# A convolution stack with an FFT-domain layer: the last sums of an image pair, moved from VectorE alone to ScalarE, VectorE and GpSimd

## The chip, the cores and the metric

One core of a Trainium2 chip runs the whole kernel. The metric is the device time of one execution in microseconds (us). The kernel before was timed in three runs: median 3791.02 us, from 3787.89 to 3796.55. A further execution was profiled; it took 3767.42 us.

## The reference

The input is a batch of 32 samples, each with 16 channels of 256 x 256 fp32 values. Two layers follow each other, both of the form x + conv(group_norm(x)):

```python
x = x + _L0_conv_ref(_gn(x), L0_conv_weight_int8, L0_conv_scale_weight, L0_conv_bias)
x = x + _L1_conv_ref(_gn(x), L1_conv_w_real, L1_conv_w_imag, L1_conv_b_real, L1_conv_b_imag)
```

Layer 0 quantises the normalised input with one scale for the whole batch (the maximum over all samples) and convolves it 3 x 3. Layer 1 goes to the frequency domain, convolves there and comes back:

```python
X = jnp.fft.rfftn(x, axes=(-2, -1), norm='backward')
Xr, Xi = (jnp.real(X), jnp.imag(X))
Yr = _rconv(Xr, wr) - _rconv(Xi, wi) + b_real[:, None, None]
Yi = _rconv(Xr, wi) + _rconv(Xi, wr) + b_imag[:, None, None]
return jnp.fft.irfftn(lax.complex(Yr, Yi), axes=(-2, -1), norm='backward')
```

## The kernel before, in words

**Layout.** The 128 partitions hold 16 channels x 8 rows. A sample is 32 blocks of 8 rows, `img[u]` (two samples in SBUF, u = 0 or 1). Two blocks make a pair, so a sample has 16 pairs (`PAIRS`).

**Setup** (about the first 680 us). Sums, squares, maxima and minima of all samples give the batch scale; GpSimd builds the weights meanwhile.

**Main stage.** `periods` runs one period per sample s, and a period has 16 slots, t = 0 to 15. In slot t each engine does its part for pairs that are at different stages:

- TensorE (PE), in this order: `turn_pair(t+4)` transposes a folded pair (L963); `dft_pair(t+3)` transforms it along the row (L972); for the next sample `row_means` (L1030) and `conv_pair` of layer 0 (L1017, L1019), of which `CONV_OF` gives slots 0 to 3 one pair, slots 4 to 9 two, and slots 10 to 15 none; `mix_pair(t+1)` applies the frequency-domain weights (L985) from `stack`; `finish_pair(t)` brings the pair back to pixels in `fin_ps` (L999, L1004), with the part that is even about the row's middle (the cosine part) in `fin_ps[:, :, 0, :]` and the odd one (the sine part) in `fin_ps[:, :, 1, :]`. In slots 4 to 9 `row_means` and `conv_pair` stand once before `mix_pair` and once behind it.
- ScalarE (ACT): `turn_out(t+4)` evicts the transposes (L540), `x_high(t+3)` the high half of the spectrum into `xn` (L547), `scale_pair` (L533), `y_high(t+1)` (L554), and `store(t-2)`, two DMAs to `out` from ACT's own queue (L562).
- VectorE (DVE): `y_low(t)` (L827), `x_low(t+3)` (L821), `layer0_pair` (L834, then statistics L836), `round_pair` (L813, L815), `finish_pair(t)` (L844 to L849).
- GpSimd (POOL): `fold(t+4)` (L729 to L732), which may run two turns ahead of PE.
- The SyncE queue (SP): `load_pair(t-3)` of the sample after next into the rows that `store` has emptied (it waits for the store's landing, L461), `restack(t+3)` (four DMAs xn to stack, L454), and `halo_rows` in slots 2, 6, 10 and 14 (L443).

**The end of a pair.** `near` are the columns 0 to 127 of the pair's rows, `far` the columns 255 down to 128. near gets even + odd, far gets even - odd. VectorE does it with four operations of 128 x 256 each, all on PSUM and `img`. The last raises `done_s`, for which PE's next `finish_pair` waits (there is one `fin_ps`), and `store` on ScalarE.

**Once per sample.** The statistics of the next sample pass through slots 10 and 11: DVE L855 and L857, PE `group_stat` (L1046) twice, DVE L870, POOL L741, DVE L877 (`zb_s`), for which `fold(16)` waits. In slots 12 to 15 the edge rows are transformed: ACT L582, L583, PE `dft_rows` (L1054, behind `finish_pair(13)`), ACT L586, DVE `row_low` (L883), PE `mix_rows` (L1065, slot 14), ACT L571, DVE L889, PE `finish_rows` (L1075), ACT L590, L591.

Each engine runs its own list in the order in which it is written; between engines there are only semaphores.

## Time and profile before

| what | before |
|---|---|
| three timed runs, median (lowest to highest) | 3791.02 us (3787.89 to 3796.55) |
| the profiled execution | 3767.42 us, span 3765.6 us |
| PE busy, instructions | 2979.5 us (79%), 45732 |
| DVE busy | 3117.7 us (83%), 5880 |
| ACT busy | 1893.1 us (50%), 2799 |
| POOL busy | 1490.4 us (40%), 1984 |
| 16 DMA engines, mean rate | 194 GB/s, 730.98 MB |
| granted TensorE clock | 0.99 of full speed |

Busy shares are means over the setup, in which PE has nothing to do, and the main stage. A busy PE is counted while a matmul is in its pipeline. The clock is full in the whole main stage.

### The profile page before, as it was taken

What the parts mean: (1) busy time and instruction counts of PE and PEld (TensorE: products, weight loads), DVE (VectorE), ACT (ScalarE), POOL (GpSimd) and SP (SyncE); (2) the same over time, 40 slices, a digit from 0 to 9 for tenths busy, and PEclk for the clock granted to TensorE, in tenths of its full rate; (3) what the DMA queues carried; (4) which work ended last, traced back from release to release, by engine and by line L of the source; (5) the groups of instructions that cost most, each with busy time, mean ns of one, the idle gap of its engine ahead of it and who ended that gap; (6) DMA issues with size and microseconds to landing.
All of it is one profiled execution on the core that took longest, in us unless ns stands there. A gap on an engine that the chain in (4) does not pass through costs nothing.

```text
span 3765.6 us, 126495 instructions
## 1 busy us (share of the span) xinstructions
PE 2979.5 (79%) x45732; PEld 2646.9 (70%) x45732; DVE 3117.7 (83%) x5880; ACT 1893.1 (50%) x2799; POOL 1490.4 (40%) x1984
## 2 busy tenths in 40 slices
PE   0000004899999999999999989999999999999998
PEld 0000002788888888888888878888888888888888
DVE  8999994688878888888888878888888888888876
ACT  8999981344444444444444434444444444444443
POOL 4777000344334344343343334333433433333444
PEclk9999999999999999999999999999999999999999
DMA  8767650366666666666666656666666666666655
GB/s 309 241 236 242 236 188 16 118 196 198 198 188 196 197 195 197 194 192 195 199 194 191 195 178 194 194 192 195 192 194 191 196 192 194 193 199 191 198 179 179
DMA packets 630696, 730.98 MB, mean 194 GB/s; under 512 B 76752, under 2 KB 602160, under 8 KB 614736
## 3 DMA queue, kind: packets, MB, share of 16 engines
q1 hardware_dynamic: 482640, 588.71, 48.6%
q10 hardware_dynamic: 147456, 134.28, 12.7%
q8 instruction: 374, 6.13, 0.7%
q14 instruction: 226, 1.85, 0.2%
HBM read 262.58 MB, written 134.22 MB: 105 GB/s over the span
## 4 chain that ended last, share of the span: by engine, by line
PE 50%; SPq 16%; issue 11%; DMA 11%; DVE 9%; ACT 1%; POOL 1%; ACTq 1%; DVEq 0%; POOLq 0%
PE y_ps L985 12%; PE mean_b L1030 10%; SPq L454 9%; PE conv_ps L1017 7%; PE x_ps L972 6%; DMA stack<-xn 5%; PE fin_ps L1004 5%; SPq L376 4%; PE t_ps L963 3%; DMA out<-img 3%; PE conv_ps L1019 3%; DVE scaled L758 2%; DMA img<-in_x 2%; PE fin_ps L999 2%; DVE scaled L759 1%
## 5 line engine op out<-in xcount | busy, mean ns | idle before, releaser
L729 POOL TENSOR_SCALAR eo<-img,norm 128x256 f32<-128x256 f32 x512 | 481.5, 940 | 1502.1 <-PE t_ps L963 1274.2
L985 PEld LDWEIGHTS y_ps<-mix_w,stack 128*128 128x128 f16 x24576 | 787.5, 99 | 158.1 <-DMA stack<-xn 84.6
L985 PE MATMUL y_ps<-mix_w,stack 128*128 128x64 f16 x24576 | 810.4, 194 | 62.4 <-DMA stack<-xn 62.0
L540 ACT ACTIVATE xt<-t_ps 128x512 f32<-128x512 f32 x512 | 305.8, 597 | 910.8 <-PE t_ps L963 802.9
L554 ACT ACTIVATE y_hi<-y_ps 128x512 f16<-128x512 f32 x512 | 305.8, 597 | 535.4 <-PE y_ps L985 534.4
L834 DVE SCALAR_TENSOR_TENSOR img<-conv_ps,cst,img 128x512 f32<-128x512 f32 x512 | 382.3, 747 | 226.9 <-PE conv_ps L1019 226.4
L821 DVE SCALAR_TENSOR_TENSOR xn<-x_ps,norm,xn 128x512 f16<-128x512 f32 x512 | 383.1, 748 | 220.7 <-ACT xn L547 215.6
L1030 PE MATMUL mean_b<-row_mean,img 128*128 128x48 f32 x4096 | 538.2, 275 | 16.6 <-DVE img L834 16.2
L972 PE MATMUL x_ps<-dft,xt 128*128 128x128 f32 x4096 | 543.0, 276 | 0.0
L1030 PEld LDWEIGHTS mean_b<-row_mean,img 128*128 128x128 f32 x4096 | 511.3, 196 | 31.7 <-DVE img L834 31.5
L972 PEld LDWEIGHTS x_ps<-dft,xt 128*128 128x128 f32 x4096 | 499.7, 192 | 0.1
L547 ACT ACTIVATE xn<-x_ps,norm 128x512 f16<-128x512 f32 x512 | 352.4, 688 | 231.0 <-DMA stack<-xn 145.3
L533 ACT ACTIVATE scaled<-img,b,a 128x512 f32<-128x512 f32 x512 | 412.0, 805 | 106.1 <-DVE quant L813 71.1
L1004 PE MATMUL fin_ps<-inv,y_hi 128*128 128x128 f16 x4096 | 459.1, 221 | 0.0
L951 PE MATMUL misc_ps<-im_f,group 128*128 128x32 f32 x2 | 0.6, 396 | 575.5 <-DVE im_f L779 575.5
L1017 PE MATMUL conv_ps<-quant,conv_w 128*128 128x512 bf16 x1536 | 427.2, 388 | 25.6 <-DMA halo<-quant 25.5
L951 PEld LDWEIGHTS misc_ps<-im_f,group 128*128 128x128 f32 x2 | 0.5, 310 | 575.5 <-issue 575.5
L1004 PE MATMUL fin_ps<-inv,y_lo 128*128 128x128 f16 x2048 | 400.6, 221 | 0.0
L1004 PEld LDWEIGHTS fin_ps<-inv,y_hi 128*128 128x128 f16 x4096 | 358.8, 99 | 39.6 <-issue 0.2
L730 POOL TENSOR_TENSOR eo<-img 128x256 f32<-128x256 f32 x512 | 381.1, 744 | 0.0
L732 POOL TENSOR_TENSOR eo<-eo,img 128x256 f32<-128x256 f32 x512 | 376.2, 735 | 0.0
L836 DVE BATCH_NORM_STATS2 bn<-img 128x6 f32<-128x512 f32 x512 | 355.6, 694 | 17.6
(134 smaller groups left out, 5138.9 us busy)
## 6 DMA issues: line engine op xcount, KB each, us to landing
stack<-xn SPq DMA_DIRECT2D x2048, 132.0 KB, 2.6
img<-in_x SPq DMA_DIRECT2D x1024, 128.0 KB, 2.8
out<-img ACTq DMA_DIRECT2D x1024, 128.0 KB, 3.0
img<-in_x SPq DMA_DIRECT2D x120, 1024.0 KB, 4.9
halo<-quant SPq DMA_DIRECT2D x192, 193.3 KB, 3.3
halo<-quant SPq DMA_DIRECT2D x64, 169.1 KB, 3.0
row_mean<-table_row_mean SPq DMA_DIRECT2D x1, 768.0 KB, 15.4
spread<-table_spread SPq DMA_DIRECT2D x1, 512.0 KB, 14.4
```

What stands on the lines that cost most here:

```text
L533: nc.scalar.activation(scaled[:], img[u][:, 2 * j:2 * j + 2, :], ACT.Identity, bias=b0[:, bass.ds(k, 1)], scale=a0[:, bass.ds(k, 1)]).then ...
L729: nc.gpsimd.tensor_scalar(even, rows[:, :, 0:F], norm[v][:, 2:3], None, ALU.add).then_inc(shift_s, 1)
L730: nc.gpsimd.tensor_tensor(odd, rows[:, :, 0:F], rows[:, :, N - 1:F - 1:-1], ALU.subtract)
L732: nc.gpsimd.tensor_tensor(even, even, rows[:, :, N - 1:F - 1:-1], ALU.add).then_inc(fold_s, 1)
L821: nc.vector.scalar_tensor_tensor(natural(t, 1), x_ps[:].rearrange("p q b k -> p (q b) k"), norm[v][:, 4:5], natural(t, 0), ALU.mult, ALU.s ...
L834: nc.vector.scalar_tensor_tensor(rows, conv_ps[:], out_scale, rows, ALU.mult, ALU.add).then_inc(x1_s, 1)
L836: nc.vector.bn_stats(bn[:, c, :], rows).then_inc(bn_s, 1)
L972: last = nc.tensor.matmul(x_ps[:, q, b, :], xt[:, t % 2, b, q, :], dft[:, q, :], start=True, stop=True)
L985: last = nc.tensor.matmul(y_ps[t % 2][:, g, b, :], stack[:, t % 2, g, first:first + F], mix_w[:, 2 * at + b, g, f, part, :], start=i == 0, ...
L1004: last = nc.tensor.matmul(fin_ps[:, b, q, :], y[:, t % 2, 2 * b + q].rearrange("p x g -> p (x g)"), inv[:, q, part, :], start=False, stop= ...
L1017: nc.tensor.matmul(conv_ps[:], conv0_w[:, dw, :], quant[:, 2 * c:2 * c + 2, dw:dw + N], start=dw == 0, stop=False)
L1030: nc.tensor.matmul(mean_ps[half], img[u][:, hb, F * half:F * half + F], row_mean[:, hb, :], start=False, stop=False)
```

## The change

ScalarE gets a new operation behind `y_high`, in front of `store`: `odd_out(t)` waits for `finish_pair(t)` of PE and copies the odd part, scaled, from `fin_ps` to SBUF (`odd_part`, four buffers). VectorE adds the even part to near and far (two operations) and now waits for that copy. GpSimd does near + odd and far - odd of pair t-2 behind `fold(t+4)`, and raises `done_s`. PE's next `finish_pair` waits for the copy (`odd_s`) and for VectorE (`even_s`), no longer for `done_s`.

```diff
+        odd_part = sb("odd_part", [P, 4, 2, F])
...
+            def odd_out(s, t):
+
+                act.wait_ge(fin_s, done(s, t))
+                act.wait_ge(done_s, done(s, t - 4))
+                nc.scalar.activation(odd_part[:, t % 4], fin_ps[:, :, 1, :], ACT.Copy, scale=1.0 / FIN).then_inc(odd_s, 1)
...
+                    if mix:
+                        odd_out(s, t)
                     if mix and t >= 2:
                         store(s, u, t - 2)
...
+            def unfold(s, u, t):
+
+                rows, odd = img[u][:, 2 * t:2 * t + 2, :], odd_part[:, t % 4]
+                near, far = rows[:, :, 0:F], rows[:, :, N - 1:F - 1:-1]
+                pool.wait_ge(even_s, done(s, t))
+                pool.sem_inc(tick_s, 1)
+                pool.wait_ge(odd_s, done(s, t))
+                pool.sem_inc(tick_s, 1)
+                nc.gpsimd.tensor_tensor(near, near, odd, ALU.add)
+                nc.gpsimd.tensor_tensor(far, far, odd, ALU.subtract).then_inc(done_s, 1)
...
                     if runs(mix, conv, t + 4):
                         fold(s, u, t + 4)
+                    if mix and t >= 2:
+                        unfold(s, u, t - 2)
+                    if later(s, mix) and t < 2:
+                        unfold(s - 1, 1 - u, t + PAIRS - 2)
...
+            for t in (PAIRS - 2, PAIRS - 1):
+                unfold(samples - 1, 1, t)
...
-                even, odd = fin_ps[:, :, 0, :], fin_ps[:, :, 1, :]
-                dve.wait_ge(fin_s, done(s, t))
-                nc.vector.scalar_tensor_tensor(near, even, 1.0 / FIN, near, ALU.mult, ALU.add).then_inc(even_s, 1)
+                even = fin_ps[:, :, 0, :]
+                dve.wait_ge(odd_s, done(s, t))
+                nc.vector.scalar_tensor_tensor(near, even, 1.0 / FIN, near, ALU.mult, ALU.add)
                 nc.vector.scalar_tensor_tensor(far, even, 1.0 / FIN, far, ALU.mult, ALU.add).then_inc(even_s, 1)
-                dve.wait_ge(even_s, 2 * (PAIRS * s + t) + 1)
-                nc.vector.scalar_tensor_tensor(near, odd, 1.0 / FIN, near, ALU.mult, ALU.add)
-                dve.wait_ge(even_s, 2 * (PAIRS * s + t) + 2)
-                nc.vector.scalar_tensor_tensor(far, odd, -1.0 / FIN, far, ALU.mult, ALU.add).then_inc(done_s, 1)
...
                 pe.wait_ge(ylo_s, done(s, t))
-                pe.wait_ge(done_s, done(s, t - 1))
+                pe.wait_ge(even_s, done(s, t - 1))
+                pe.wait_ge(odd_s, done(s, t - 1))
```

What stands on ScalarE in a row where slots 4 to 9 follow each other, before (`scaled` is the pair for the quantisation, `xt` the transposes, `y_hi` the mixed spectrum's high half):

```order
L533 ACTIVATE scaled<-img,b,a 128x512 [waits rounded_s]
L554 ACTIVATE y_hi<-y_ps 128x512 [waits fin_s,mix_s]
L562 ISA [waits done_s]
L562 DMA out<-img 16x8x256
L562 ISA
L562 DMA out<-img 16x8x256
L538 REGISTER_ALU
L540 ACTIVATE xt<-t_ps 128x512 [waits dft_s,t1_s]
```

and now:

```order
L534 ACTIVATE scaled<-img,b,a 128x512 [waits rounded_s]
L555 ACTIVATE y_hi<-y_ps 128x512 [waits fin_s,mix_s]
L561 ACTIVATE odd_part<-fin_ps 128x256 [waits done_s,fin_s]
L569 ISA [waits done_s]
L569 DMA out<-img 16x8x256
L569 ISA
L569 DMA out<-img 16x8x256
L539 REGISTER_ALU
L541 ACTIVATE xt<-t_ps 128x512 [waits dft_s,t1_s]
```

The two DMAs of the store stood behind the wait for `mix_s` alone; now they stand behind a wait for `fin_s` too, which is the end of PE's slot.

The same engine in slot 13, now, where the edge rows of the next sample pass (`row_n` waits for `dft_rows`, which PE does behind `finish_pair(13)`):

```order
L555 ACTIVATE y_hi<-y_ps 128x512 [waits fin_s,mix_s]
L593 ACTIVATE row_n<-misc_ps,norm 48x2x128 [waits rowx_s]
L561 ACTIVATE odd_part<-fin_ps 128x256 [waits done_s,fin_s]
L569 ISA [waits done_s]
L569 DMA out<-img 16x8x256
```

`odd_part` is new there, behind `row_n`; the store already stood behind `row_n` before.

VectorE in slots 13 and 14, now (the odd copy gives `odd_s`):

```order
L871 SCALAR_TENSOR_TENSOR img<-fin_ps,img 128x2x128 [waits odd_s]
L872 SCALAR_TENSOR_TENSOR img<-fin_ps,img 128x2x128
L854 TENSOR_TENSOR y_lo<-y_ps,y_hi 128x512 [waits yhi_s]
L906 SCALAR_TENSOR_TENSOR row_n<-misc_ps,norm,row_n 48x2x128 [waits rowxh_s]
L848 SCALAR_TENSOR_TENSOR xn<-x_ps,norm,xn 128x4x128 [waits xhi_s]
```

Four additions on `fin_ps` have become two, and the first of them waits for ScalarE instead of PE.

## Rows read from the trace of the kernel before

**Rows 1.** Busy time by window: slot 5 of a sample; slots 10 to 15
```profile
1600.47:1607.57 7.10, 7.10 (x102) 6.12 (x100) 6.01 (x13) 2.58 (x4) 2.30 (x3) 1.00 0.50 154
1630.94:1662.74 31.80, 27.38 (x501) 25.58 (x500) 23.83 (x64) 15.69 (x30) 16.29 (x21) 1.00 0.62 188
```
(The columns are: us; then busy us of PE, PEld, DVE, ACT, POOL; clock; DMA share; GB/s.)

**Rows 2.** Who waited for whom, 768 to 3700 us: total, times, longest
```profile
PE y_ps L985 <- DMA stack<-xn: 57.9, 61, 2.4
PE t_ps L963 <- POOL eo L732: 47.6, 31, 1.7
PE misc_ps L1046 <- DVE small L857: 33.7, 30, 1.1
```

**Rows 3.** The SyncE queue's own waits, whole span
```profile
SPq L462 <- DMA out<-img: 166.9, 161, 2.9
```

**Rows 4.** Timeline of slot 5 (slots 6 to 9 alike): start, us, what
```profile
1600.47 0.22 PE L1004 MATMUL fin_ps<-inv,y_lo 128*128 128x128 f16 x1
1601.17 0.60 ACT L540 ACTIVATE xt<-t_ps 128x512 f32<-128x512 f32 x1 [2.51 <-PE t_ps L963]
1601.23 0.41 DVE L844 SCALAR_TENSOR_TENSOR img<-fin_ps,img 128x256 f32<-128x256 f32 x1
1602.06 0.69 ACT L547 ACTIVATE xn<-x_ps,norm 128x512 f16<-128x512 f32 x1 [0.30 <-PE x_ps L972]
1602.55 0.68 DVE L827 TENSOR_TENSOR y_lo<-y_ps,y_hi 128x512 f16<-128x512 f32 x1
1603.14 0.75 DVE L821 SCALAR_TENSOR_TENSOR xn<-x_ps,norm,xn 128x512 f16<-128x512 f32 x1
1603.80 0.75 DVE L834 SCALAR_TENSOR_TENSOR img<-conv_ps,cst,img 128x512 f32<-128x512 f32 x1
1604.93 0.64 PEld L1030 LDWEIGHTS mean_b<-row_mean,img 128*128 128x128 f32 x5
1605.16 0.60 ACT L554 ACTIVATE y_hi<-y_ps 128x512 f16<-128x512 f32 x1 [1.71 <-PE y_ps L985]
1605.36 1.27 ACTq L562 DMA_DIRECT2D out<-img  x2
```

**Rows 5.** Timeline of a slot in which DVE was late
```profile
1589.94 0.74 DVE L834 SCALAR_TENSOR_TENSOR img<-conv_ps,cst,img 128x512 f32<-128x512 f32 x1
1590.74 0.41 PEld L1030 LDWEIGHTS mean_b<-row_mean,img 128*128 128x128 f32 x3 [0.77 <-DVE img L834]
```

**Rows 6.** Timeline, PE in slots 10 and 12: the statistics
```profile
1632.36 0.61 PE L1046 MATMUL misc_ps<-small,group 128*128 128x1 f32 x4 [1.12 <-DVE small L857]
...
1640.90 0.55 PE L963 MATMUL t_ps<-ident,eo 128*128 128x128 f32 x3 [1.56 <-POOL eo L732]
```

**Rows 7.** Timeline of slots 13 and 14: the edge rows
```profile
1650.35 0.42 DVE L844 SCALAR_TENSOR_TENSOR img<-fin_ps,img 128x256 f32<-128x256 f32 x1 [0.24 <-PE fin_ps L1004]
1651.36 0.47 ACT L586 ACTIVATE row_n<-misc_ps,norm 48x256 f16<-48x256 f32 x1 [1.30 <-PE misc_ps L1055]
1652.28 0.47 DVE L883 SCALAR_TENSOR_TENSOR row_n<-misc_ps,norm,row_n 48x256 f16<-48x256 f32 x1
1652.81 1.19 PE L1065 MATMUL misc_ps<-image_w,row_n 48*128 48x96 f16 x24
1653.00 0.60 ACT L540 ACTIVATE xt<-t_ps 128x512 f32<-128x512 f32 x1 [1.17 <-PE x_ps L972]
1653.49 0.68 ACT L547 ACTIVATE xn<-x_ps,norm 128x512 f16<-128x512 f32 x1
1654.21 0.75 DVE L821 SCALAR_TENSOR_TENSOR xn<-x_ps,norm,xn 128x512 f16<-128x512 f32 x1 [1.46 <-ACT xn L547]
```

**Rows 8.** Groups by line: shape, count, busy, mean ns of one, idle before
```profile
L732 POOL TENSOR_TENSOR eo<-eo,img 128x256 f32<-128x256 f32 x512 | 376.2, 735 | 0.0
L591 ACT ACTIVATE im_f<-misc_ps 128x128 f32<-128x128 f32 x32 | 8.6, 269 | 0.0
```

**Rows 9.** Timeline, DVE beside a busy POOL
```profile
1644.38 0.70 DVE L815 TENSOR_SCALAR quant<-quant 128x512 bf16<-128x512 bf16 x1
```

More of the change, by code:

```diff
@@ L295, in build @@
             "images_s"))
-        fold_s, t1_s, t1e_s, dft_s, xhi_s, xlo_s, mix_s, yhi_s, ylo_s, fin_s, even_s, done_s = (sem(n) for n in (
-            "fold_s", "t1_s", "t1e_s", "dft_s", "xhi_s", "xlo_s", "mix_s", "yhi_s", "ylo_s", "fin_s", "even_s", "done_s"))
+        fold_s, t1_s, t1e_s, dft_s, xhi_s, xlo_s, mix_s, yhi_s, ylo_s, fin_s, even_s, odd_s, done_s = (sem(n) for n in (
+            "fold_s", "t1_s", "t1e_s", "dft_s", "xhi_s", "xlo_s", "mix_s", "yhi_s", "ylo_s", "fin_s", "even_s", "odd_s", "done_s"))
         shift_s = sem("shift_s")
@@ L495, in _ @@
             act.sem_inc(p1_act, 8)
-            for q in (t1e_s, xhi_s, yhi_s):
+            for q in (t1e_s, xhi_s, yhi_s, odd_s):
                 act.sem_inc(q, LEAD)
@@ L607, in _ @@
             pool.sem_inc(fold_s, LEAD)
+            pool.sem_inc(done_s, LEAD)
             setup = Tally(pool, setup_p)
@@ L744, in _ @@
             periods(pool, period)
+            for t in (PAIRS - 2, PAIRS - 1):
+                unfold(samples - 1, 1, t)
         @block.vector
         def _(dve):
-            for q in (xlo_s, ylo_s, done_s, x1_s):
+            for q in (xlo_s, ylo_s, even_s, x1_s):
                 dve.sem_inc(q, LEAD)
```

## The prediction

> **What bounds the kernel now.** I read the page first: PE and DVE are both near 80% busy, with no work for PE in the setup. So shares do not decide, and I went to windows, waits and timelines of one sample (some 97 us, 16 slots).
>
> In a slot with two conv pairs PE is busy for all of its 7.10 us and DVE for 6.01 [rows 1]: PE is the bound there, six slots in sixteen, and a faster DVE buys nothing. In slots 10 to 15 PE is busy for 27.38 of 31.80 us: the idle time that can be won lies there and in the slots just behind. Its largest parts are waits for the restacked spectrum, 57.9 us in total, for the first fold of the next sample, 47.6, and for the first statistic, 33.7 [rows 2]. Only the last two hang on DVE. The first hangs on SP, which itself stood 166.9 us waiting for stores to land before it could load [rows 3]. So the whole idle time of PE that any change could win is about 140 us, and what DVE can give is a part of 81.
>
> Call F the moment at which PE's `finish_pair` is done. In rows 4 it is 1600.47 + 0.22 plus 0.04 = 1600.73.
>
> **The change part by part.**
>
> *VectorE* loses two of four additions. Four take 1602.55 - 1601.23 = 1.32 us from start to start, so two free 0.66 us a slot [rows 4]. But the first now waits for ScalarE's copy. No row shows a copy of 256 PSUM columns; 128 take 269 ns [rows 8] and 512 take 0.60 us [rows 4], and between these I take 0.38. Copy from F to F + 0.38, VectorE at F + 0.42: before, it began at F + 0.50, held by other work. So in long slots the wait costs nothing and `y_low` starts at F + 1.1 instead of F + 1.82.
>
> *ScalarE's queue.* This is where I expect the cost. `store` was issued behind `y_high`: in rows 4 at 1605.36, while ScalarE had nothing to do until the next slot's transposes. Now it is issued behind the copy, so at F + 0.2, and `turn_out` stands behind it. The store's two DMA issues take 1.27 us [rows 4]; from the operation ahead of a store to the `turn_out` behind it pass 1653.00 - 1651.36 = 1.64 us [rows 7]. So `turn_out` starts at F + 1.65, where it started at F + 0.44 [rows 4].
> What is queued behind it: `x_high` 0.49 later [rows 7], at F + 2.14; `x_low` on VectorE 0.72 behind that [rows 7], at F + 2.86, where it was at F + 2.41; `layer0_pair` 0.66 later [rows 4], at F + 3.52; and PE's weight load for `row_means` can start 0.80 after that [rows 5], at F + 4.32. PE was there at 1604.93, F + 4.20 [rows 4]. So PE stalls 0.12 us in each long slot when both issues are quick. The 0.66 us that VectorE saves are used up in waiting for `x_high`. Store issues are not all quick, and a stalled PE also loses the overlap of its first weight load; I take 0.2 us. The lower bound is nothing (the issues overlap more than I think), the upper is the 0.77 of the late slot [rows 5]. Long slots: 6 x 31 samples = 186, at 0.2: **+37 us** (0 to +143).
>
> For this the Trainium skill has a rule that speaks the other way ("DMA: Bandwidth & Descriptors", Issuing engines are not separate DMA queues): starting DMAs from several engines saves only sequencer time, which is usually small beside the DMA. By it, moving the store in ScalarE's list would be free, and this term 0. The trace differs here: 1.27 us of issuing on an engine whose next work is on PE's path.
>
> *Edge rows.* In slot 13 the copy stands behind `row_n`, which starts at 1651.36 [rows 7]. The copy then starts at about 1651.76, VectorE at 1652.2 (it was 1650.35), `y_low` at 1652.85, `row_low` at 1653.45 (it was 1652.28): 1.17 us later, and PE's `mix_rows` began 0.53 us behind `row_low`, nearly unwaited [rows 7]. 31 x 1.17 = **+36 us**, if nothing behind takes it up.
>
> *Statistics.* Slot 10: `y_low`, L855 and L857 come 0.66 us earlier, and PE waits 1.12 for them [rows 6]: -0.66. Slot 11 to 12: the chain to `zb_s` passes one more `finish_pair` of VectorE, at which VectorE used to arrive just as PE finished; with the copy ahead it saves between 0 and 0.66, I take 0.35; PE waits 1.56 at its end [rows 6]. Together 31 x 1.0 = **-31 us**.
>
> *SP's queue.* Stores land later against PE's slots: by about 2.6 us in long slots (F + 0.2 instead of 1605.36 for a slot that ends at 1607.8), by 0.9 in short ones (`y_high` starts that much before F there). In long slots SP has time. From slot 10 on SP is nearly without pause, so `load_pair` and then `restack` move by some 0.3 us, and PE's waits for the stack [rows 2] are what is late next. They take part of what the statistics give (their gain arrives at a stack that is not earlier), about 0.8 us a sample, and they also swallow most of the 1.17 us of the edge rows, since SP does not wait for PE there: the later slots 15, 0 and 1 wait that much less for the stack, about 1.1. Net of these: +0.3 + 0.8 - 1.1 = 0 a sample, within -0.5 and +2 (SP's wait for stores is 5 us a sample now). **0 us** (-15 to +60).
>
> *GpSimd.* Two more operations of 735 ns [rows 8], 1.5 us a slot on 2.30 [rows 1]: 3.8 in slots of 5 to 7 us. It runs two turns ahead, so I cost it at nothing. The cover is thinnest behind `fold(16)`: fold, unfold, fold are 2.3 + 1.5 + 2.3 us, against two turns of PE in some 10. *PE's new waits* (copy and even part) end earlier than `done_s` did: nothing. *The end*: copy, two additions and two operations of GpSimd instead of four additions: +1.5 us once.
>
> Sum: 37 + 36 - 31 + 0 + 1.5 = 43.5, **+44 us**, to 3811 against the profiled execution's 3767. The runs' median is 3791, 0.6% above the profiled one; 44 us is 1.2%, so **3835 us**.
>
> **The rivals.**
> *Faster.* The long slots lose nothing (the 0.12 us is within what rows show for one slot), and of the 1.17 us of the edge rows the stack waits take 1.1 while the statistics' 1.0 stays, because SP keeps up. Per sample -1.0 + 1.17 - 1.1 = -0.9, -29 us: 3762. For it: the slack in the long slots is missed by a tenth of a us only, and stores no longer leave together with the restack DMAs. Against: SP's waits [rows 3]. It decides where the store's issue costs ScalarE less than 1.5 us.
> *SP becomes the bound.* Every store's landing moves SP: the 0.9 us of short slots reach `mix_pair` in three or four of the ten short slots: 31 x 3 = +93 on top of 37: 3921. For it: the 166.9 us [rows 3]. Against: most of it is in long slots, where SP only waits early.
> *Port contention.* L815 takes 0.30 us mostly and 0.70 while GpSimd is busy [rows 9]. With GpSimd busy 1.65 times as long, some 30 us more of VectorE, half of them beside PE's waits: +15, to 3850 with the rest. The Trainium skill ("SBUF — State Buffer") says that one of VectorE and GpSimd fully blocks while the other holds the shared port; the trace agrees in kind with the 0.70.
> *No change that can be told.* Long slots keep their slack and the other terms cancel (36 - 31): 3791 to 3798.
>
> **How the numbers follow.** A measurement can tell about 0.2%, 7.6 us. My forecast (slower, 3800 to 3880, port contention included) has 0.50; SP as the bound 0.13; no change 0.14; faster 0.23. So faster 0.23, same 0.14, slower 0.63. The range from 3766 to 3895 leaves out about 0.1 at either end.
>
> **What would show it.** Right: `turn_out` some 1.2 us later against F in long slots; their length 7.2 to 7.4 us instead of 7.10, with PE waits on L1030's line for DVE; `mix_rows` waiting about 1 us for `row_low`; the wait for the first statistic down to about 0.5; DVE's busy time down by some 425 us without the span following. Wrong: long slots still 7.10 us, or SP's waits for stores growing by more than 60 us.

## The result, and the profile after

The changed kernel takes 3893.88 us (median of four runs, 3883.99 to 3906.98); the kernel before, on the same chip, 3789.45. The ratio (of the means) is 1.0284, with a 95% interval of 1.0235 to 1.0333. So it is slower by 2.8%; the medians lie 104 us apart. The forecast had the direction, but its 3835 was only 44 us above the kernel before. The profiled execution took 3883.99 us (span 3882.2, against 3765.6 before: 117 us more), at a granted clock of 0.991 (0.992 before). The two clocks are alike as means; where the clock falls is not alike, as shown below.

The page of the kernel after: busy time of the engines; the chain that ended last; groups of instructions (busy us, mean ns of one, idle time before it and what ended it).

```profile
PE 3012.6 (78%) x45732; PEld 2663.8 (69%) x45732; DVE 2923.2 (75%) x4856; ACT 2041.3 (53%) x3311; POOL 2221.8 (57%) x3008
...
PE 46%; DMA 13%; SPq 13%; issue 12%; DVE 8%; ACTq 4%; ACT 3%; POOL 0%; DVEq 0%; POOLq 0%
...
L561 ACT ACTIVATE odd_part<-fin_ps 128x256 f32<-128x256 f32 x512 | 196.3, 383 | 563.8 <-PE fin_ps L1028 561.1
L840 DVE TENSOR_SCALAR quant<-scaled 128x512 bf16<-128x512 f32 x512 | 293.0, 572 | 16.6 <-ACT scaled L534 11.3 <-issue 0.4
L842 DVE TENSOR_SCALAR quant<-quant 128x512 bf16<-128x512 bf16 x512 | 212.3, 415 | 17.6
```

VectorE lost two of four additions a slot and 194.5 us of busy time (3117.7 before), and the kernel became slower. DMA and SP's queue (SPq) hold a quarter of the chain that ended last, but they held 27% of it before, so this tells nothing. New in the chain are ScalarE's DMA issues (ACTq, 4% where it was 0%) and ScalarE itself (3% where it was 1%): that is the first hint. The second is a comparison of the waits, with [rows 2] for the kernel before. The kernel after, who waited for whom, 768 to 3800 us (total, times, longest); lines have moved, so L1008 is `mix_pair`, L986 `turn_pair`, L1089 `mix_rows`, L1041 `conv_pair`, L1070 `group_stat`, L1099 `finish_rows`, L1054 `row_means`:

```profile
PE y_ps L1008 <- DMA stack<-xn: 53.6, 41, 3.0
...
PE t_ps L986 <- POOL eo L742: 34.9, 31, 1.2
...
PE misc_ps L1089 <- DVE row_n L906: 33.6, 30, 1.1
...
PE conv_ps L1041 <- DMA halo<-quant: 26.7, 17, 3.0
PE misc_ps L1070 <- DVE small L880: 26.1, 30, 0.9
PE misc_ps L1099 <- DVE iy_lo L912: 25.5, 27, 2.0
...
PE mean_b L1054 <- DVE img L861: 18.0, 37, 1.1
```

Three of [rows 2] are there again (the first fold and the statistic shorter by 12.7 and 7.6 us), and four waits have grown from nearly nothing: for the edge rows' `row_low`, for the halo rows of layer 0, for `iy_lo` and for layer 0's result. SP's own waits, whole span, against [rows 3]:

```profile
SPq L463 <- DMA out<-img: 452.6, 215, 6.0
...
SPq L449 <- PE y_ps L1008: 52.1, 29, 5.3
...
SPq L467 <- DMA out<-img: 28.2, 34, 3.0
```

SP waits 481 us for stores to land, where it waited 170. It used to wait 234.5 us for PE before it restacked, and that spare time is down to 52.1.

One slot in detail. I averaged the time from one `finish_pair` to the next on PE over samples 3 to 28, by slot, from the starts and lengths in the two traces (us):

```
slot     0    1    2    3    4    5    6    7    8    9   10   11   12   13   14   15   sum
before 5.82 6.27 5.46 5.39 7.35 7.14 7.10 7.22 7.10 7.10 7.12 3.64 5.77 4.10 6.15 4.40  97.1
after  6.57 5.62 5.37 5.34 7.47 7.24 7.25 8.73 7.48 7.37 6.42 3.62 5.41 5.88 7.26 3.78 100.8
```

A sample takes 3.7 us more; 31 samples make 115 of the 117 us. Four places stand out: slot 7 (+1.51), slot 13 (+1.78), slot 14 (+1.11) and slot 0 (+0.75).

Not all of this is waiting. I had written ahead of the prediction that the clock is full in the whole main stage. It is not: for short stretches the granted clock falls from its full level (2.4 GHz) to the half one (1.2 GHz). Slot 10 of two samples of the kernel before, a stretch inside the second, and slot 10 of the kernel after (columns as in [rows 1], the clock is third from the end):

```profile
1629.08:1635.72 6.64, 5.52 (x92) 5.37 (x91) 5.12 (x16) 2.58 (x4) 0.56 (x1) 1.00 0.39 123
2210.34:2218.56 8.22, 7.10 (x92) 6.90 (x91) 5.37 (x16) 2.58 (x4) 0.85 (x1) 0.79 0.38 118
2215.00:2217.50 2.50, 2.50 (x35) 2.44 (x33) 0.15 (x2) 0.60 (x1) 0.00 (x0) 0.50 0.00 0
```
```profile
1666.81:1673.20 6.39, 5.52 (x92) 5.37 (x91) 4.87 (x14) 2.86 (x5) 1.97 (x3) 1.00 0.43 131
```

In the kernel before, slot 10 takes 6.64 us in 18 of the 26 samples, at full clock, and 8.09 to 8.24 in the other 8. There the clock falls to half 0.9 to 1.6 us behind the end of PE's wait for the first statistic (1.12 us in every sample), and the slot takes some 1.5 us more. In the kernel after that wait is 0.87 us, and no half-clock stretch begins in slot 10. They begin elsewhere: of 17 in its main stage, 7 in slot 7 and 9 in slot 13, mostly right behind PE's waits for the halo rows and the stack. The sum has changed little (51 us of the main stage at half clock before, 65 after), but its place has.

The timeline of a long slot, after (start, us, what; in brackets the idle time before). Here F, the end of `finish_pair`, is 1659.38 + 0.22 + 0.04 = 1659.64:

```profile
1659.38 0.22 PE L1028 MATMUL fin_ps<-inv,y_lo 128*128 128x128 f16 x1
...
1659.63 0.38 ACT L561 ACTIVATE odd_part<-fin_ps 128x256 f32<-128x256 f32 x1 [2.07 <-PE fin_ps L1028]
...
1659.84 1.28 ACTq L569 DMA_DIRECT2D out<-img  x2
...
1660.79 0.68 DVE L854 TENSOR_TENSOR y_lo<-y_ps,y_hi 128x512 f16<-128x512 f32 x1
...
1661.28 0.60 ACT L541 ACTIVATE xt<-t_ps 128x512 f32<-128x512 f32 x1 [1.26 <-PE x_ps L995]
...
1661.78 0.68 ACT L548 ACTIVATE xn<-x_ps,norm 128x512 f16<-128x512 f32 x1
...
1662.49 0.75 DVE L848 SCALAR_TENSOR_TENSOR xn<-x_ps,norm,xn 128x512 f16<-128x512 f32 x1 [1.02 <-ACT xn L548]
...
1663.16 0.74 DVE L861 SCALAR_TENSOR_TENSOR img<-conv_ps,cst,img 128x512 f32<-128x512 f32 x1
...
1663.95 0.97 PEld L1054 LDWEIGHTS mean_b<-row_mean,img 128*128 128x128 f32 x8
```

ScalarE stands 1.26 us in front of `turn_out` (L541). The row names `x_ps` as what it waited for, but the two store issues (L569) fill just this gap: the label is only the last semaphore seen. `turn_out` starts at F + 1.64 (it was F + 0.44), `x_low` (L848) at F + 2.85, and PE's weights for `row_means` at F + 4.31. `y_lo` is early, at F + 1.15, and VectorE then stands 1.02 us for `x_high`.

And a slot in which SP comes too late. SP's queue, then PE, then the chain through them:

```profile
1639.98 1.39 SPq L377 DMA_DIRECT2D img<-in_x  x2
1641.62 2.70 SPq L455 DMA_DIRECT2D stack<-xn  x4
1644.51 1.35 SPq L444 DMA_DIRECT2D halo<-quant  x2
...
1648.93 0.73 PE L1041 MATMUL conv_ps<-quant,conv_w 128*128 128x512 bf16 x2 [1.63 <-DMA halo<-quant]
```
```profile
1634.86 0.57 ACTq L569
1635.60 4.16 DMA out<-img
1639.98 0.61 SPq L377
...
1645.14 3.55 DMA halo<-quant
```

The store issued at 1634.86 lands at 1639.76. SP waits for that before it loads (L377), and its queue runs in order: four restack DMAs and two halo DMAs stand behind. The eight issues take some 0.7 us each, the halo rows leave at 1644.5 to 1645.9, land at 1648.69, and PE has waited 1.63 us.

### The profile page after: what moved, and what is told of

It reads as the page before. It is cut to its first block, busy times and chain, and to the rows that moved or that the text cites. A ratio compares the mean times of both kernels' runs of the same rounds, so it can differ in the third digit from the quotient of the medians.

```text
span 3882.2 us, 127689 instructions
## 1 busy us (share of the span) xinstructions
PE 3012.6 (78%) x45732; PEld 2663.8 (69%) x45732; DVE 2923.2 (75%) x4856; ACT 2041.3 (53%) x3311; POOL 2221.8 (57%) x3008
## 4 chain that ended last, share of the span: by engine, by line
PE 46%; DMA 13%; SPq 13%; issue 12%; DVE 8%; ACTq 4%; ACT 3%; POOL 0%; DVEq 0%; POOLq 0%
PE y_ps L1008 11%; PE mean_b L1054 8%; PE conv_ps L1041 7%; PE fin_ps L1028 6%; SPq L455 6%; DMA out<-img 5%; PE x_ps L995 5%; ACTq L569 4%; DMA stack<-xn 4%; SPq L377 3%; PE t_ps L986 2%; PE conv_ps L1043 2%; DVE scaled L785 2%; PE fin_ps L1023 2%; DMA img<-in_x 2%
## 5 line engine op out<-in xcount | busy, mean ns | idle before, releaser
L752 POOL TENSOR_TENSOR img<-img,odd_part 128x256 f32<-128x256 f32 x512 | 378.3, 739 | 1082.7 <-DVE img L872 1082.4
L1008 PEld LDWEIGHTS y_ps<-mix_w,stack 128*128 128x128 f16 x24576 | 786.5, 99 | 149.5 <-DMA stack<-xn 75.8
L1008 PE MATMUL y_ps<-mix_w,stack 128*128 128x64 f16 x24576 | 807.4, 193 | 60.0 <-DMA stack<-xn 59.4
L848 DVE SCALAR_TENSOR_TENSOR xn<-x_ps,norm,xn 128x512 f16<-128x512 f32 x512 | 383.9, 750 | 496.3 <-ACT xn L548 494.9
L541 ACT ACTIVATE xt<-t_ps 128x512 f32<-128x512 f32 x512 | 305.9, 597 | 671.4 <-PE x_ps L995 537.4
L1054 PE MATMUL mean_b<-row_mean,img 128*128 128x48 f32 x4096 | 541.4, 276 | 31.9 <-DVE img L861 30.9
L1054 PEld LDWEIGHTS mean_b<-row_mean,img 128*128 128x128 f32 x4096 | 510.6, 196 | 56.1 <-DVE img L861 51.4
L561 ACT ACTIVATE odd_part<-fin_ps 128x256 f32<-128x256 f32 x512 | 196.3, 383 | 563.8 <-PE fin_ps L1028 561.1
L1041 PE MATMUL conv_ps<-quant,conv_w 128*128 128x512 bf16 x1536 | 428.6, 389 | 54.4 <-DMA halo<-quant 49.7
L742 POOL TENSOR_TENSOR eo<-eo,img 128x256 f32<-128x256 f32 x512 | 388.9, 759 | 0.0
L753 POOL TENSOR_TENSOR img<-img,odd_part 128x256 f32<-128x256 f32 x512 | 382.1, 746 | 0.0
```

The source lines that it names most:

```text
L742: nc.gpsimd.tensor_tensor(even, even, rows[:, :, N - 1:F - 1:-1], ALU.add).then_inc(fold_s, 1)
L752: nc.gpsimd.tensor_tensor(near, near, odd, ALU.add)
L753: nc.gpsimd.tensor_tensor(far, far, odd, ALU.subtract).then_inc(done_s, 1)
L848: nc.vector.scalar_tensor_tensor(natural(t, 1), x_ps[:].rearrange("p q b k -> p (q b) k"), norm[v][:, 4:5], natural(t, 0), ALU.mult, ALU.s ...
L1008: last = nc.tensor.matmul(y_ps[t % 2][:, g, b, :], stack[:, t % 2, g, first:first + F], mix_w[:, 2 * at + b, g, f, part, :], start=i == 0, ...
L1041: nc.tensor.matmul(conv_ps[:], conv0_w[:, dw, :], quant[:, 2 * c:2 * c + 2, dw:dw + N], start=dw == 0, stop=False)
```

## The experiments

Theory A: the loss is the late store, which lands later, so that SP comes late, and whose two issues hold `turn_out` on ScalarE. Theory B: it is the place of the copy, behind the pieces of the edge rows. Theory C: it is VectorE and GpSimd slowing each other. From e5 on theory A is taken apart: A1 is the landing, through SP's queue, and A2 the issue, on ScalarE. All experiments compute the whole reference. Each ratio is against executions of the kernel before that were taken beside it (medians of 3784 to 3788 us).

**e1_store_first.** The changed kernel, with the store back in front of the copy:

```diff
-                    if mix:
-                        odd_out(s, t)
                     if mix and t >= 2:
                         store(s, u, t - 2)
                     if later(s, mix) and t < 2:
                         store(s - 1, 1 - u, t + PAIRS - 2)
+                    if mix:
+                        odd_out(s, t)
```

> The changed kernel, with the store back in front of the odd copy, behind y_high and the edge-row pieces, as before the change. Theory A (the store stands behind the end of PE's slot: it lands later, and SP, which loads and restacks only behind that landing, comes late; and its two issues hold turn_out): the halo wait of slot 7 (1.0 us a sample in the changed kernel), the long slots' 0.1 to 0.4 us and most of the stack wait of slot 13 go, 2.5 to 3.5 us a sample, 80 to 110 us: ratio to the kernel before 0.998 to 1.008; SP waits for stores back under 220 us. Theory B (the loss is the odd copy behind the edge-row pieces): ratio 1.022 to 1.028. Theory C (VectorE and GpSimd hold each other up: quantisation 216 to 293 us and 179 to 212 us in the changed kernel, and GpSimd's list is longer): ratio above 1.022 too, with the edge rows' wait as it was.

Measured: 3847.44 us, 1.0170 [1.0146, 1.0194]. PE's waits, 768 to 3780 us:

```profile
PE misc_ps L1089 <- DVE row_n L906: 73.9, 31, 2.6
...
PE fin_ps L1023 <- DVE y_lo L854: 39.5, 34, 1.8
```

That lies between A (0.998 to 1.008) and B and C (from 1.022), so none of them holds alone. The long slots are at 7.10 to 7.19 us again and SP waits 172 us for stores, both as before the change. But slot 14 grew to 9.65 us, and 20 of the 22 half-clock stretches of the main stage begin there: in slot 13 the copy now stands behind `row_n` and behind the store's issues too, and VectorE (additions, `y_lo`, `row_low`) behind the copy. So the store's place is worth 1.1% as it stands, and the copy's place still costs more than that.

**e2_copy_ahead_of_rows.** The changed kernel, with the copy ahead of the edge rows' pieces; the store stays late:

```diff
                     if runs(mix, conv, t + 1):
                         y_high(s, t + 1)
+                    if mix:
+                        odd_out(s, t)
                     if conv and t == IMAGE_AT:
...
-                    if mix:
-                        odd_out(s, t)
                     if mix and t >= 2:
                         store(s, u, t - 2)
```

> The changed kernel, with the odd copy right behind y_high, ahead of the edge-row pieces of slots 12, 13 and 15; the store stays behind all of them. Theory B: PE's waits for row_low (1.12 us a sample in slot 14) and most of those for iy_low (0.79 in slot 15 to 0) go, 1.5 to 1.9 us a sample, about 50 us: ratio 1.013 to 1.017. Theory A: the waits go, but the queue of SP is behind there and PE waits for the stack instead; the ratio moves by less than half of that, 1.020 to 1.026. Theory C: unchanged.

Measured: 3873.81 us, 1.0238 [1.0211, 1.0265], in the range given for A. Slot 14 is back to 6.16 us, but the total moved only 0.5%, and the interval overlaps that of the change:

```profile
PE y_ps L1008 <- DMA stack<-xn: 86.5, 63, 3.1
```

The waits for the stack rose from 53.6 to 86.5 us, most of it in the slots 15, 0 and 1. Of the 1.1 us that slot 14 gave back a sample, PE spent most in waiting for SP.

**e3_both.** The order `y_high`, store, copy, edge rows' pieces:

```diff
                     if runs(mix, conv, t + 1):
                         y_high(s, t + 1)
+                    if mix and t >= 2:
+                        store(s, u, t - 2)
+                    if later(s, mix) and t < 2:
+                        store(s - 1, 1 - u, t + PAIRS - 2)
+                    if mix:
+                        odd_out(s, t)
                     if conv and t == IMAGE_AT:
```

> Both: order on ScalarE is y_high, store, odd copy, edge-row pieces. If A and B are the two causes and add up, what is left is the gain of the statistics (0.7 + 0.4 us a sample in the changed kernel, 34 us): ratio 0.985 to 0.998. Under theory C it stays above 1.01, since nothing on VectorE or GpSimd is changed.

Measured: 3764.77 us, 0.9948 [0.9932, 0.9965]. The loss is gone, and a half per cent is won, which theory C did not allow (above 1.01). The two places are no terms of a sum: the copy's place alone brings 0.5%, the store's alone 1.1%, both 3.4%. Each hides the other: with a late store the time that slot 14 gives back becomes a wait for the stack, and with an early store the copy that stands behind `row_n` also waits out the issues. The half per cent (19 us) is not less waiting: PE's listed waits are 5.2 us a sample, as before (5.1). It goes with the clock, on which more behind e11.

**e4_before_late_store.** The kernel before, with its four additions on VectorE, and only the store made late. If the late store is the cause, this is as slow as the change:

```diff
+                    if mix:
+                        act.wait_ge(fin_s, done(s, t))
+                        act.sem_inc(tick_s, 1)
                     if mix and t >= 2:
                         store(s, u, t - 2)
```

> The kernel before, with one thing added: ahead of each store ScalarE waits for PE's finish_pair of the running slot (fin_s), which is where the changed kernel issues it. No arithmetic is moved. Theory A: the halo wait of slot 7, the stack wait of slot 13 and the long slots' stalls appear here too: ratio 1.015 to 1.028. Theories B and C: 0.998 to 1.004.

Measured: 3907.0 us, 1.0318 [1.0297, 1.0340]. SP's waits, 768 to 3780 us:

```profile
SPq L462 <- DMA out<-img: 468.3, 213, 6.1
SPq L448 <- PE y_ps L988: 8.1, 7, 4.8
```

This is more than the 1.015 to 1.028 expected under A, and B and C (to 1.004) are out as the main cause. One wait makes a loss as large as the change's, with no copy and nothing new on GpSimd; slot 7 takes 8.74 us as in the change (8.73). So a late store is enough. It is not the same loss in every slot: slot 14 grows by 0.20 us here and by 1.11 in the change, where the copy stands behind `row_n` (e2 shows that this is the copy's place), and slot 10 stays at 7.19 where the change has 6.42. That the change stands lower, at 1.0284, is within the two intervals.

A late store can cost in two ways: its issue holds ScalarE, and its landing holds SP. The next four move the load, and only that, to the end of SP's slot, behind the DMAs that PE waits for:

```diff
+                    if runs(mix, conv, t + 3):
+                        restack(s, t + 3)
+                    if t in (2, 6) and conv:
+                        halo_rows(s + 1, t // 4 + 2)
+                    if t in (10, 14) and ahead:
+                        halo_rows(s + 2, t // 4 - 2)
                     if mix and t >= 3 and ahead:
                         sp.wait_ge(store_s[(t - 3) % STORES], stored(s, t - 3))
...
                         load_pair(s + 1, 1 - u, t + PAIRS - 3)
-                    if runs(mix, conv, t + 3):
-                        restack(s, t + 3)
-                    if t in (2, 6) and conv:
-                        halo_rows(s + 1, t // 4 + 2)
-                    if t in (10, 14) and ahead:
-                        halo_rows(s + 2, t // 4 - 2)
```

**e5_after_load_last.** The changed kernel with this edit.

> The changed kernel, with SP's load_pair moved behind restack and halo_rows in each slot, so that these no longer stand behind the wait for a store's landing; ScalarE is as changed. Theory A1 (of the store's lateness it is the landing that costs, through SP's queue): the halo wait of slot 7 and the stack wait of slot 13 go, 2.5 us a sample; left are the long slots (0.1 to 0.3 each), the edge rows and iy_low: ratio 1.003 to 1.012. Theory A2 (it is the issue, which holds turn_out and x_high on ScalarE): ratio 1.020 to 1.028, long slots and edge rows as they were and the stack wait only moved.

Measured: 3797.66 us, 1.0029 [1.0016, 1.0042]. PE's waits, 768 to 3780 us:

```profile
PE misc_ps L1089 <- DVE row_n L906: 35.5, 31, 1.4
...
PE y_ps L1008 <- DMA stack<-xn: 27.1, 26, 2.5
...
PE misc_ps L1099 <- DVE iy_lo L912: 24.2, 27, 1.9
```

This is at the lower edge of A1 (1.003 to 1.012) and far from A2 (from 1.020). 96 us are gone; by the mean granted clock (0.997 here, 0.990 in the change) some 27 of them are clock. The wait for halo rows is gone and that for the stack is halved: slot 7 takes 7.55 us (8.73), slot 13 4.41 (5.88). The waits that hang on ScalarE's queue stay as they were: slot 14 at 7.27, slot 0 at 6.52, the other long slots at 7.26 to 7.37.

**e6_before_late_store_load_last.** e4's edit and this one together, on the kernel before.

> The kernel before with the store made late (1.032 in its own run), with SP's load_pair behind restack and halo_rows. A1: 1.003 to 1.012, with the long slots' 0.1 to 0.3 us left. A2: 1.022 to 1.032.

Measured: 3828.75 us, 1.0108 [1.0086, 1.0130], in the range of A1; long slots 7.39 to 7.47 us.

**e7_before_load_last.** The control: this edit alone on the kernel before.

> Control: the kernel before, with SP's load_pair behind restack and halo_rows and nothing else. The stack waits (57.9 us in total in the kernel before) shrink: A1 0.985 to 0.998. If a later load makes scale_pair late, above 1.002.

Measured: 3756.13 us, 0.9910 [0.9887, 0.9933], as expected; the long slots 6, 8 and 9 stay at 7.10 us. So SP's order is worth 0.9% by itself; where, the two profiles do not show (spans of 3763.0 and 3765.6 us, and PE's wait for the stack 49.6 us where the kernel before has 61.6 in the same stretch). With SP out of the way, a late store still costs 1.0108 / 0.9910, 2.0%; with the load ahead of the restack it costs 3.2% (e4). On the kernel before, then, I read 2.0% of it as issue (the slots 5, 6, 8 and 9 are longer than in e7 by 0.29 to 0.36 us, 4 and 7 by 0.17 and 0.25, and the edge rows' chain comes later) and 1.2% as landing. On the changed kernel the edit brings 2.5%, 0.9 of which the control has too, so some 1.6% is the later landing. Both splits take for granted that the parts add up, which e1 to e3 show is not always so.

**e8_both_load_last.** e3's list for ScalarE with this edit for SP.

> Order on ScalarE y_high, store, odd copy, edge-row pieces (0.9948 in its own run), with SP's load_pair last. If the stack waits left in it (1.6 us a sample in slots 13 to 3) are SP's queue: 0.980 to 0.990; if they are the time of the restack's own DMAs, no change, 0.993 to 0.997.

Measured: 3748.79 us, 0.9900 [0.9879, 0.9921]. That is the upper edge of the 0.980 to 0.990 expected if SP's queue makes the stack waits (29.3 us now, 49.9 in e3). It is not below e7 (0.9910, intervals overlap): the split's gain is not to be seen. The trace names what eats it, the copy behind the store's issues (VectorE's wait, 768 to 3780 us):

```profile
DVE img L871 <- ACT odd_part L561: 269.8, 261, 5.4
```

**e9_store_ahead_of_y_high.** e8, with the store one place further up, in the time in which ScalarE waits for PE's `mix_pair` anyway:

```diff
-                    if runs(mix, conv, t + 1):
-                        y_high(s, t + 1)
                     if mix and t >= 2:
                         store(s, u, t - 2)
                     if later(s, mix) and t < 2:
                         store(s - 1, 1 - u, t + PAIRS - 2)
+                    if runs(mix, conv, t + 1):
+                        y_high(s, t + 1)
```

> As e8, with the store one place earlier on ScalarE, ahead of y_high, where in long slots ScalarE waits for PE anyway (1.7 us). In e8 the odd copy still stands right behind the store's issues, and VectorE waited 252 us for it. If the issue time matters wherever something urgent stands behind it: that wait falls under 120 us, the row_low wait (0.70 us a sample) under 0.3, ratio 0.980 to 0.987 (e8: 0.990). If only the landing matters, the stores land some 1.8 us earlier, where SP (load last) no longer needs it: 0.988 to 0.992.

Measured: 3735.08 us, 0.9865 [0.9846, 0.9883], the fastest of all. Waits in the same stretch:

```profile
DVE img L871 <- ACT odd_part L561: 97.5, 125, 4.1
...
PE y_ps L1008 <- DMA stack<-xn: 67.1, 68, 2.7
```

The first row was 269.8 us in e8. `row_low` no longer holds PE (0.5 us in all) and slot 14 takes 6.09 us, all as expected if the issue time matters. What is left are the three waits of [rows 2], with 67.1 us for the stack, 37.4 for the first fold and 26.1 for the statistic.

**e10_before_load_last_busy_pool.** Theory C by itself: e7 with two more GpSimd operations of the same shape behind each fold, on a tile of their own that nobody reads:

```diff
+                nc.gpsimd.tensor_tensor(idle[:, 1], idle[:, 0], idle[:, 0], ALU.add)
+                nc.gpsimd.tensor_tensor(idle[:, 2], idle[:, 0], idle[:, 0], ALU.subtract)
```

> As e7 (the kernel before with load_pair last, 0.991), with two more operations of 128 x 256 on GpSimd behind each fold, from and to a scratch tile that nothing reads. Theory C (VectorE's quantisation is held up by GpSimd): the two quantisation groups go from 216 and 179 us to some 260 to 290 each; if that is on the path, ratio 0.996 to 1.005; if it lies in VectorE's slack, 0.989 to 0.994.

Measured: 3756.04 us, 0.9917 [0.9902, 0.9933], against 0.9910 for e7. VectorE's quantisation is lengthened, and the time stays:

```profile
L817 DVE TENSOR_SCALAR quant<-scaled 128x512 bf16<-128x512 f32 x512 | 242.1, 473 | 16.6 <-ACT scaled L534 11.3 <-issue 0.4
L819 DVE TENSOR_SCALAR quant<-quant 128x512 bf16<-128x512 bf16 x512 | 196.6, 384 | 17.6
```

This lengthens the pair by 43 us, less than the 110 of the change and less than I had planned (to 260 to 290 us each), so by itself it is a weak test. But e9 has more of it than the change (280.2 + 273.3 us, 158 more than before) and is the fastest kernel, and e4 has the loss without any of it. As the cause of the loss theory C falls. That the lengthening costs nothing is not shown; of one short operation the last section shows that it does.

**e11_before_store_early_load_last.** The other control: both better orders without the split (e7 with the store ahead of `y_high`).

```diff
+                    if mix and t >= 2:
+                        store(s, u, t - 2)
+                    if later(s, mix) and t < 2:
+                        store(s - 1, 1 - u, t + PAIRS - 2)
                     if runs(mix, conv, t + 1):
                         y_high(s, t + 1)
...
-                    if mix and t >= 2:
-                        store(s, u, t - 2)
-                    if later(s, mix) and t < 2:
-                        store(s - 1, 1 - u, t + PAIRS - 2)
```

> As e7, with the store ahead of y_high, as in e9: VectorE keeps all four additions. Control for e9: the difference of the two is what the split of the sums itself gives. Expected 0.986 to 0.992, so 0.3 to 0.8% for the split (the statistics' 0.7 us a sample is 0.6%).

Measured: 3751.58 us, 0.9916 [0.9898, 0.9933]. So of e9's 1.35%, 0.5% comes with the split of the additions (0.9865 against 0.9916, intervals apart). The rest e7 has with SP's order alone (0.9910); the early store adds nothing to it on the kernel before.

**How the split gives its half per cent.** "Short of full clock" is an estimate, (1 - granted clock) x time, from the mean clock of each kernel's timed runs; the last two columns are from its trace (samples 3 to 28; main stage).

| kernel | granted clock | short of full clock | PE's listed waits, a sample | half-clock stretches that begin in slot 10 |
|---|---|---|---|---|
| before | 0.990 | 38 us | 5.12 us | 10 |
| the change | 0.990 | 40 us | 7.50 us | 0 |
| e3 | 0.995 | 18 us | 5.21 us | 0 |
| e7 | 0.992 | 32 us | 4.56 us | 19 |
| e8 | 0.997 | 12 us | 4.51 us | 0 |
| e9 | 0.997 | 10 us | 4.64 us | 0 |
| e11 | 0.992 | 29 us | 4.50 us | 11 |

PE waits no less in e9 than in e11: the 0.25 and 0.34 us that it waits less in slots 10 and 12 come back in slots 13 and 15 as waits for the stack (0.48 and 0.19). What differs is the clock, by some 18 us, and the medians differ by 16.5. In all six kernels with four additions on VectorE (before, e4, e6, e7, e10, e11) PE waits 1.12 us for the first statistic, and in 9 to 19 of 31 samples the clock then falls to half; in all seven with the split it waits 0.87 us there and the clock falls in none. So the split pays by a clock that does not fall, more than by the time it takes off VectorE. That the shorter wait is the reason is my reading; no run changes that wait alone.

Not tried: VectorE adding the even part without waiting for the copy. In e9 it stands 97.5 us for it. Both would read `fin_ps` at the same time. The Trainium skill ("Advanced Engine Details and Errata", Bank Collisions) says that TensorE, VectorE and ScalarE cannot access the same PSUM bank within the same partition on the same cycle; no run here shows whether that would come into play, or what it would cost.

## Why the prediction was right and where it was wrong

**ScalarE's queue in long slots: right.** Forecast: `turn_out` at F + 1.65, `x_low` at F + 2.86, PE's weight load at F + 4.32. Measured in the slot above: F + 1.64, 2.85, 4.31. Forecast 0.2 us a slot. The slots 4 to 6, 8 and 9 grew by 0.12, 0.10, 0.15, 0.38 and 0.27, and slot 7 by 0.33 where SP is out of the way (e5): 1.35 a sample, +42 us against +37. (Some 0.1 of slot 8's 0.38 is clock, a half-clock stretch that runs over from slot 7: in e5 it grew by 0.24.)

**Edge rows: right.** 1.17 us forecast, slot 14 grew by 1.11 (+34 us against +36). The rows of one such place, after:

```profile
1691.07 0.47 ACT L593 ACTIVATE row_n<-misc_ps,norm 48x256 f16<-48x256 f32 x1 [2.33 <-PE misc_ps L1079]
1691.44 0.36 ACT L561 ACTIVATE odd_part<-fin_ps 128x256 f32<-128x256 f32 x1
1691.84 0.42 DVE L871 SCALAR_TENSOR_TENSOR img<-fin_ps,img 128x256 f32<-128x256 f32 x1 [3.02 <-ACT odd_part L561]
...
1693.11 0.47 DVE L906 SCALAR_TENSOR_TENSOR row_n<-misc_ps,norm,row_n 48x256 f16<-48x256 f32 x1
1693.63 0.77 PE L1089 MATMUL misc_ps<-image_w,row_n 48*128 48x96 f16 x14 [1.12 <-DVE row_n L906]
```

**Statistics: right in sum, by luck.** Slots 10 and 12 lost 0.70 and 0.36 us (0.66 and 0.35 forecast), -33 us against -31. Slot 12 is as forecast. But in slot 10 the wait for the first statistic fell by only 0.25 a sample (1.12 to 0.87), not by 0.66: see L880 in the last section. The other 0.45 is the clock, which the forecast had as full: 8 of 26 slots were 1.5 us longer for a half-clock stretch before, and none after. Two errors of like size cancelled.

**SP's queue: here the forecast failed.** The step was "Net of these: +0.3 + 0.8 - 1.1 = 0 a sample", resting on "In long slots SP has time" and, against the rival in which SP becomes the bound, "most of it is in long slots, where SP only waits early". The -1.1 came: slots 15 and 1 lost 0.62 and 0.65. The costs that stand against it were not 1.1 but 2.96: slot 13 grew by 1.78 and slot 7 by 1.51, of which 0.33 is the long slots' part (e5). With small changes of slots 2, 3 and 11 (-0.16) the net is 2.96 - 1.27 - 0.16 = 1.5 a sample, +47 us, within the bounds of that term (-15 to +60) but not the 0 that I took. SP had no time in long slots. It waited there for PE, 234.5 us in all, but a load that waits for a landing 2.9 us later (11.6 us behind the start of its slot, where it was 8.7) holds six more DMAs, and in slot 6 two of them are the halo rows that PE needs in slot 7. I had counted SP's spare time by slot and not by what stands last in its queue. The sign of being wrong that I had named came too: SP's waits for stores grew by 311 us, and the limit was 60. The rival in which SP becomes the bound had the right cause and the wrong places and size: it looked to the short slots (31 x 3), and 1.18 of the 2.96 came in slot 7, a long one.

A second thing is in this term that neither the forecast nor the rival had. PE's waits for the stack and the halo rows grew by only 0.6 us a sample in sum (2.12 to 2.72). In slots 7 and 13 there also begin 16 half-clock stretches in 31 samples, where one began before. At 1.5 us each, as slot 10 shows them, I estimate that at 0.8 us a sample: about half of the term's 1.5 is clock, behind PE's new waits.

**`iy_lo`: not seen.** The edge rows' second step passes slot 15, and there it stands in the same chain as in the long slots. On ScalarE `turn_out` comes out behind the late store's issues, then `x_high`; on VectorE `iy_lo` stands behind `x_low`, which waits for `x_high`; and `finish_rows` waits:

```profile
1697.46 1.29 ACTq L569 DMA_DIRECT2D out<-img  x2
...
1700.42 0.75 DVE L848 SCALAR_TENSOR_TENSOR xn<-x_ps,norm,xn 128x512 f16<-128x512 f32 x1 [1.40 <-ACT xn L548]
...
1701.59 0.28 PE L1099 MATMUL misc_ps<-inv,iy_hi 128*128 128x128 f16 x2 [0.75 <-DVE iy_lo L912]
```

`iy_lo` starts 0.6 us later behind the start of slot 15 than before (4.07 against 3.48 us), and slot 15 has become 0.62 shorter. The copy has no part in it: e4, without a copy, has the same wait (23.6 us), and `y_lo` comes earlier than before. Slot 0 grew by 0.75 us, +23 us. It stayed in e5 (6.52) and is gone in e9 (5.77). The order of VectorE's list in slot 15 would have shown it.

The terms as measured, from the slot averages: 42 + 34 - 33 + 47 + 23 = 113, with 1.5 at the end 115, against 117 in the spans.

The forecast failed in size, then, in two terms that I had at nothing: SP's queue (+47 us) and `iy_lo` (+23 us). The others came near.

**The other rivals.** "Faster" was to decide itself by whether the store's issue costs ScalarE less than 1.5 us. It cost 1.28, and long slots lost time all the same: the chain behind it comes out at F + 4.31, and PE was there at F + 4.20, so that condition was drawn too wide. Port contention came larger than forecast (110 us more in the two quantisation operations, not 30) and no run shows that these two operations cost time; the one-column addition of the last section did cost some, 0.4 us a sample in PE's wait. "DVE's busy time down by some 425 us" was wrong: 194.5. Additions start 0.33 us apart although each lasts 0.41, so two fewer save 0.66 a slot, 338 us, and the lengthened operations take 110 and more back. The wait for the first statistic was to fall to about 0.5 us and fell to 0.87.

**The rule of the Trainium skill** that was weighed ("DMA: Bandwidth & Descriptors", Issuing engines are not separate DMA queues: the issue time is usually small relative to the DMA) would have made this move free. The rule speaks of starting DMAs from several engines; that it would hold for a place in one engine's list was my reading. By the runs it is not: with SP's part taken out, the moved issue costs 2.0% (e6 against e7). Beside the DMA it is no trifle either, 1.28 us for two issues against 3.0 us to landing.

## What to carry to other kernels

A DMA that moves down one engine's list moves twice: its issue now stands ahead of whatever follows on that engine, and its landing comes later for whoever waits, with everything queued behind that waiter. Read the waiter's queue to its last item and ask which of them PE needs first; put what waits for a landing behind what others wait for. When work is split over engines, place the new producer (here the copy) ahead of every wait that is not its own, or the engine that got lighter will stand and wait for it; and two such misplacements may hide each other, so that mending one alone (0.5%, 1.1%) says little about mending both (3.4%). And look at the granted clock by slot before you add up waits: here a wait of PE could bring a half-clock stretch worth 1.5 us behind it, more than the wait itself (1.12 us).

## What the runs showed of the hardware

VectorE's quantisation operations became longer while GpSimd did more: 422 to 572 ns and 350 to 415 ns on average in the change, 545 and 557 in e3_both, though shapes and types are the same. In the trace of the change, the second of them takes 298 to 304 ns in all 307 cases in which no GpSimd operation runs when it starts. In the 85 cases that start beside `fold`'s last addition (L742) its median is 704 ns, and it ends 0.16 us behind that addition. A one-column addition went from 160 to 558 ns on average (some 570 in 31 of 32 cases). The average, and one case beside GpSimd's operation:

```profile
L880 DVE TENSOR_TENSOR small<-small,cst 128x1 f32<-128x1 f32 x32 | 17.8, 558 | 1.1
```
```profile
1467.37 0.73 POOL L753 TENSOR_TENSOR img<-img,odd_part 128x256 f32<-128x256 f32 x1
1467.54 0.57 DVE L880 TENSOR_TENSOR small<-small,cst 128x1 f32<-128x1 f32 x1
```

It starts 0.17 us into GpSimd's subtraction and ends 0.01 to 0.02 us behind its end.

It was L857 before (160 ns), it stands in PE's wait for the first statistic, and it took back 0.4 of the 0.66 us that VectorE came earlier. In e10, where GpSimd's extra work stands right behind each fold and GpSimd is idle at that moment, it stayed at 159 ns. So it depends on what GpSimd does at that moment. The Trainium skill ("SBUF — State Buffer", Who interferes with whom) says that a VectorE instruction with two SBUF inputs contends with a GpSimd instruction that reads SBUF, that one in a 2-port mode contends with GpSimd too, and that the shared ports are an exclusive lock. The one-column addition has two SBUF inputs, and its ends just behind GpSimd's agree with that. Whether the quantisation runs in a 2-port mode no run here shows.
